# Cross-attention on one core: three score banks, paired value tiles, row sums in a maximum buffer, one transpose for the negated maxima

## What is computed

```python
x = (hidden_states - mu) * jax.lax.rsqrt(var + LN_EPS) * ln_gamma + ln_beta
Q = _split_heads(x @ Wq.T)          # B=2, 32 heads, 512 rows, 32 columns
K = _split_heads(memory_keys)       # 1024 rows; memory_keys = memory_values = ctx_4096
V = _split_heads(memory_values)
scores = jnp.einsum('bhsd,bhtd->bhst', Q, K) * scale
scores = jnp.where(mask, scores, -jnp.inf)
probs = jax.nn.softmax(scores, axis=-1)
attn = jnp.einsum('bhst,bhtd->bhsd', probs, V)
out = attn.transpose(0, 2, 1, 3).reshape(B, S, HIDDEN) @ Wout.T
return residual + out
```

## Time and profile before

| | |
|---|---|
| median of 3 runs | 747.28 us (745.67 to 748.48) |
| the profiled execution's own time | 746.45 us |
| its span | 744.6 us |
| its mean granted TensorE clock | 0.974 |
| busy: PE, DVE, POOL, ACT | 695.1, 483.7, 391.5, 350.1 us |

### The profile page before, as it was taken

One profiled execution on the slowest core, in us unless ns is written; L12 is line 12 of the kernel. 1 busy time (PEld: TensorE's weight loads), 2 busy tenths in 40 slices (PEclk: granted clock), 3 DMA queues, 4 the chain that ended last, 5 costly groups with the idle time before them and its releaser, 6 DMA issues.

```text
span 744.6 us, 10855 instructions
## 1 busy us (share of the span) xinstructions
PE 695.1 (93%) x3585; PEld 400.3 (54%) x3585; DVE 483.7 (65%) x496; ACT 350.1 (47%) x613; POOL 391.5 (53%) x106
## 2 busy tenths in 40 slices
PE   2599999968999999999999999999999999699998
PEld 2478788633444444444444444444444444378886
DVE  6743343148688878878788787887888677732231
ACT  3732111434466666666666566665666666400000
POOL 1000000047296797967979769787796798800000
PEclk9599999979999999999999999999999999989999
DMA  9521000425326144162451523515325104131331
GB/s 346 138 71 57 29 28 1 101 66 127 93 66 156 39 120 115 48 151 52 104 132 50 131 69 89 137 48 127 88 70 128 58 1 135 36 114 57 113 113 56
DMA packets 39518, 68.10 MB, mean 91 GB/s; under 512 B 5284, under 2 KB 21798, under 8 KB 39470
## 3 DMA queue, kind: packets, MB, share of 16 engines
q1 hardware_dynamic: 39444, 67.64, 33.2%
q10 hardware_dynamic: 36, 0.01, 0.0%
HBM read 25.18 MB, written 4.19 MB: 39 GB/s over the span
## 4 chain that ended last, share of the span: by engine, by line
PE 85%; DVE 6%; SPq 5%; DMA 2%; issue 1%; ACT 1%; ACTq 0%; DVEq 0%
PE SX L894 18%; PE MX L874 17%; PE PV L910 16%; PE MX L1038 12%; PE SM L900 6%; PE PV L844 6%; PE SM L844 5%; DVE mx L701 2%; PE MX L821 2%; SPq L301 2%; DVE stats L635 1%; PE MX L815 1%; PE MX L886 1%; SPq L303 1%; DMA PR<-in_x 1%
## 5 line engine op out<-in xcount | busy, mean ns | idle before, releaser
L701 DVE TENSOR_REDUCE mx<-MX 128x1 f32<-128x1024 f32 x256 | 303.0, 1220 | 137.5 <-PE MX L874 137.2
L585 ACT ACTIVATE PR<-SX 128x512 f32<-128x512 f32 x512 | 277.5, 594 | 187.0 <-PE SX L894 186.8
L468 POOL TENSOR_TENSOR acc<-acc,PR 128x2048 f32<-128x2048 f32 x64 | 293.3, 4583 | 31.6 <-ACT PR L585 25.1
L468 POOL TENSOR_TENSOR acc<-PR 128x2048 f32<-128x2048 f32 x16 | 73.3, 4579 | 226.1 <-ACT PR L585 147.6
L894 PE MATMUL SX<-R 99*128 99x512 f32 x512 | 180.2, 432 | 2.4 <-ACT PR L585 1.6
L874 PE MATMUL MX<-R 97*128 97x512 f32 x512 | 164.1, 417 | 14.9 <-DVE mx L701 7.2
L894 PEld LDWEIGHTS SX<-R 99*128 99x128 f32 x512 | 88.4, 189 | 112.0 <-ACT PR L585 91.7
L874 PEld LDWEIGHTS MX<-R 97*128 97x128 f32 x512 | 89.2, 189 | 102.7 <-DVE mx L701 65.0
L910 PE MATMUL PV<-PR,C 128*32 128x512 f32 x1024 | 138.4, 613 | 0.1
L1038 PE MATMUL MX<-R 128*128 128x512 f32 x192 | 46.8, 404 | 5.6 <-DVE R L780 5.6
L789 DVE TENSOR_TENSOR PR<-PR,MX 128x512 f32<-128x512 f32 x16 | 11.0, 687 | 58.6 <-PE MX L1038 57.2
(11 more groups left out here) (75 smaller groups left out, 523.1 us busy)
## 6 DMA issues: line engine op xcount, KB each, us to landing
R<-KTh SPq DMA_DIRECT2D x64, 256.0 KB, 4.2
PR<-in_x SPq DMA_DIRECT2D x16, 512.0 KB, 4.1
C<-in_ctx SPq DMA_DIRECT2D x16, 512.0 KB, 3.5
R<-KTl SPq DMA_DIRECT2D x64, 128.0 KB, 3.8
R<-QT SPq DMA_DIRECT2D x64, 128.0 KB, 2.5
acc<-in_L_xattn_Wq SPq DMA_DIRECT2D x8, 512.0 KB, 3.4
R<-QT SPq DMA_DIRECT2D x64, 64.0 KB, 2.1
C<-in_L_xattn_Wout SPq DMA_DIRECT2D x8, 512.0 KB, 3.3
```

Of the source, the lines that this page charges most:

```text
L468: nc.gpsimd.tensor_tensor(acc[:, :, :], a, PR[:, tt % RING, :, :], ALU.add).then_inc(pool_used, 1)
L585: nc.scalar.activation(PR[:, tt % RING, h, :], SX[h % 2][:, :], ACT.Exp, scale=SCALE).then_inc(exp_done, 1)
L701: nc.vector.tensor_reduce(mx[:, u % 2, c:c + 1], MX[par][:, :], mybir.AxisListType.X, ALU.max, negate=True).then_inc(mx_freed, 1)
```

## The change

- Three score banks SX in turn, (4 tt + h) % 3, in place of two; the third is the bank of SM, which is gone.
- The tables go by slots of two tiles (A, B, C, D in this text: tiles 0 and 1, 2 and 3, 4 and 5, 6 and 7). A slot has its 8 scores in groups of 3, 1, 2 and 2 (`GROUPED`), each with its items behind it, and one value block behind all, with two tiles: 1 and 2, 3 and 4, 5 and 6. Tile 7 of the step before and tile 0 are done at the end of slot A, on both sides of the row sums.
- Row sums are made once per step there, as an item `sums` in an MX buffer: tiles 6 and 7 and `acc` in a row. GpSimd adds tiles 0 to 5.
- The maxima lie in the order in which they are made, so one transpose serves the bias; its rows are 16 x 128 in place of 4 x 512.
- The items are placed anew: the bias item stands at the head of slot D in place of the middle of tile 6, a step makes M6 to M15 for n+1 and M0 to M5 for n+2, in place of M4 to M15 and M0 to M3.

```diff
-POOL_TILES = (0, 1, 2, 4, 5, 6)
+BANKS = 3
+PROBS = TT * HPG
+POOL_TILES = (0, 1, 2, 3, 4, 5)
+DIRECT_TILES = (6, 7)
 ADDS = len(POOL_TILES) - 1
-SUM_SLOT = 1
-FIRST_DIRECT = min(set(range(TT)) - set(POOL_TILES))
+SLOTS = TT // 2
+
+GROUPED = [((0, 0), (0, 1), (0, 2)), ((0, 3),), ((1, 0), (1, 1)), ((1, 2), (1, 3))]
-SUMS_AT = (2, 5, 7)
-LAST_SUMS_AT = (2, 3, 4)
+SUMS_AT = ((1, 0), (1, 1))
...
 STEP = [
-    ([], keys(2)),
-    (maxima(1, 4), maxima(1, 5, 6)),
-    ([], maxima(1, 7, 8)),
-    ([], maxima(1, 9, 10)),
-    (maxima(1, 11), maxima(1, 12, 13)),
-    ([], maxima(1, 14, 15)),
-    ([], maxima(2, 0) + bias(1)),
-    (maxima(2, 1), maxima(2, 2, 3)),
+    (keys(2), maxima(1, 6), maxima(1, 7), maxima(1, 8) + sums(-1)),
+    (maxima(1, 9), maxima(1, 10), maxima(1, 11), maxima(1, 12)),
+    (maxima(1, 13), maxima(1, 14), maxima(1, 15), maxima(2, 0)),
+    (bias(1) + maxima(2, 1), maxima(2, 2), maxima(2, 3), maxima(2, 4, 5)),
 ]
...
-    BTh = sb("BTh", [HPG, S], F32R)
-    BTl = sb("BTl", [HPG, S], F32R)
-
-
-    mx = sb("mx", [P, 2, (ST - 1) * HPG + P], F32)
+    BTh = sb("BTh", [M_ITEMS, P], F32R)
+    BTl = sb("BTl", [M_ITEMS, P], F32R)
+
+
+    mx = sb("mx", [P, 2, P], F32)
...
-    SX = [nc.alloc_psum_tensor(f"SX{i}", [P, S], F32) for i in range(2)]
+    SX = [nc.alloc_psum_tensor(f"SX{i}", [P, S], F32) for i in range(BANKS)]
     PV = nc.alloc_psum_tensor("PV", [P, S], F32)
-    SM = nc.alloc_psum_tensor("SM", [P, S], F32)
-    QP = [PV, SM]
+    QP = [PV, SX[2]]
...
-            def step(n, u, items, at, first=False):
-                for tt in range(TT):
-                    exps(n, u, tt, 0)
-                    if tt == 0 and not first:
+            def step(n, items, at, first=False):
+                for k, slot in enumerate(items):
+                    for group, part in zip(GROUPED, slot):
+                        for b, h in group:
+                            exp(n, 2 * k + b, h)
+                        at = high_and_bias(n, part, at)
+                    if k == 0 and not first:
                         pv_copy(n - 1)
-                    at = high_and_bias(n, items[tt][0], at)
-                    exps(n, u, tt, 1)
-                    at = high_and_bias(n, items[tt][1], at)
...
+                            if kind == "wout":
+                                wout_parts(i, at % 2)
+                            if kind == "max":
+                                maximum(n + a, u + a, i, at % 2)
+                            if kind == "sums":
+                                invert_sums(n + a, 0, MX[at % 2][:, 0:S])
+                                dve.wait_ge(sums_turned, n + a + 1)
+                                dve.sem_inc(mx_freed, 1)
+                            at += 1
+                        if (k, j) in SUMS_AT and not first:
+                            invert_sums(n - 1, 1 + SUMS_AT.index((k, j)))
...
             def bias_item(n, u, par):
-                for st in range(ST):
-                    ins = nc.tensor.transpose(MX[par][:, st * P:(st + 1) * P], mx[:, u % 2, st * HPG:st * HPG + P], ident[:, :])
-                ins.then_inc(bt_ready, 1)
+                nc.tensor.transpose(MX[par][:, 0:P], mx[:, u % 2, :], ident[:, :]).then_inc(bt_ready, 1)
...
+
+                if at >= BANKS:
+                    pe.wait_ge(exp_done, PROBS * n + at - BANKS + 1)
+                elif not is_first(n):
+                    pe.wait_ge(exp_done, PROBS * n - PROBS + max(b for b in range(PROBS) if b % BANKS == at) + 1)
+                elif SX[at] is QP[1]:
+                    pe.wait_ge(q_copied, 2 + BATCH * GROUPS)
...
+            def row_sums(n, bank):
+
+                for tt in DIRECT_TILES:
+                    sum_probs(bank, lambda h: PR[:, tt % RING, h, :], tt == DIRECT_TILES[0], False).then_inc(tile_used, 1)
                 pe.wait_ge(pool_used, ADDS * n + 2 * ADDS)
-                sum_probs(lambda h: acc[:, h, :], False, True).then_inc(sums_done, 1)
+                sum_probs(bank, lambda h: acc[:, h, :], False, True).then_inc(sums_done, 1)
...
+                for k, slot in enumerate(items):
+                    for j, (group, part) in enumerate(zip(GROUPED, slot)):
+                        for b, h in group:
+                            score(n, u, 2 * k + b, h)
+                        if j == len(slot) - 1 and k == 0 and not first:
+                            for item in part[:-1]:
+                                mx_item(*item)
+                            values(n - 1, u + RING - 1, TT - 1)
+                            mx_item(*part[-1])
                         else:
...
+                            for item in part:
+                                mx_item(*item)
+                    if k > 0:
+                        values(n, u, 2 * k - 1)
+                    values(n, u, 2 * k)
...
-            last_sum(STEPS - 1)
+            row_sums(STEPS - 1, SX[0][:, :])
```

192 lines of the change are left out of this document (74 added, 118 removed).

## The result

The changed kernel takes 841.79 us, the median of 4 runs (837.04 to 846.47); the kernel before, run beside it, takes 746.67 us. The ratio is 1.127, with a 95% interval of 1.123 to 1.130: 95 us slower, where 53 were forecast, and 6 us above the range of 768 to 836. The profiled execution took 837.04 us.

The account below looks back on a forecast made before the run. PE was taken as the bound in steps 1 to 13. A step of 34.4 us against 30.3 gave 13 x 4.1 = 53 us on 746.45, so 800 us; forecast 788 to 818, 8-in-10 range 768 to 836.

Parts of the forecast that it names:

- The walk through the slots: One step priced slot by slot: A 10.6, B 6.5, C 6.3, D 9.3, sum 32.7 us, 5.9 of it standstill.
- The standstill behind the keys: Slot A: PE waits 1.4 us for the keys' buffer, until ACT's and DVE's copies of the keys are done.
- the one behind the bias: Slot D: PE stands still 1.8 us before the second item behind the bias, until ACT copies and DVE subtracts.
- M0's wait: Slot C: M0 waits for stacking DMAs queued behind the values' load, 1.0 us plus 0.7 for the load's traffic.
- DVE's split of the queries: Slot A: DVE's splitting of the queries was priced at 3.0 us, keeping DVE busy until 2.8.
- The clock falls as well: Rival: standstills lower PE's clock once to twice in each step, 17 to 34 us more, 817 to 834; chance 0.17.
- the whole block behind each stretch keeps PE busy: Argument against a clock fall after slot D's stretch of half-busy PE, a fall priced at 1.3 us each.
- Step 0 gains fewer borders and meets the same two waits: 0: Step 0: savings at block borders and the waits behind bias and keys were taken to give no net change.
- the clean step: Steps 1 to 13 without M0's wait or clock falls: 32.7 us each, against 30.3 before.
- PE's work: PE's own work in a step after the change, without waits: 26.8 us, 2.6 less than before.
- POOL's chain: Five POOL adds, then exponential, score, item and blocks: 29.3 us a step, deciding if both waits are covered; 731 us, chance 0.08.

Follow-up runs that it names:

- b1: Kernel before with only the bias item moved, from tile 6 to tile 7 right ahead of M1: 796.14 us, ratio 1.067.
- x1: Changed kernel with the values' load placed behind the 16 stacking DMAs in SP's queue: 803.36 us, ratio 1.076.
- x13: x10 with the values' load put back ahead of the stacking DMAs: 791.08 us, ratio 1.059.
- x9: Changed kernel with DVE's split of the queries (cast and subtraction) on one column in place of 512: 840.14 us, ratio 1.125.
- x3: x1 with the bias item also moved to the end of slot C, ahead of the value block: 800.41 us, ratio 1.075.
- x4: x3 with the keys item moved to the end of slot D and M5 to slot A: 821.13 us, ratio 1.100.
- x7: x3 with each maximum over 512 of its 1024 columns, which leaves out work: 785.21 us, ratio 1.051.
- x5: x4 with M0 to M2 placed behind the first eight scores of step 0: 816.64 us, ratio 1.092.
- x12: x10 with each maximum over 512 of its 1024 columns, which leaves out work: 741.87 us, ratio 0.993.
- x10: x5 with the queries split behind M8 of slot A, where POOL is idle, and key rows stacked first: 753.74 us, ratio 1.009.

## Why the prediction was right in sign and wrong in size

**Right: who becomes late.** The walk through the slots held, where the clock doesn't fall. Against 10.6, 6.5, 6.3 and 9.3 stand 10.88, 6.50, 6.39 and 8.82, a step of 32.6 where 32.7 was written. So close a sum is partly luck. The standstill behind the keys was put at 1.4 and is 1.39, but the one behind the bias was put at 1.8 and is 0.88. I had costed the bias rows of 16 x 128 at nothing, with the 0.59 and 0.68 of the old shape; ACT's copy takes 0.25 now and DVE's subtraction 0.28:

```profile
450.20 0.28 DVE L709 TENSOR_TENSOR BTl<-MX,BTh 16x128 fp32r<-16x128 f32 x1 [4.44 <-ACT BTh L550]
```

POOL's first add waits longer, the row sums and their blocks run as one piece of 4.4 (463.21 to 467.64), SP stacks behind the load. b1 shows the slot D standstill to be enough by itself. M0's wait, "1.7" a step, is 2.0 in 12 steps (24.1 us), and x1 and x13 show that it comes from the load's place in SP's queue. Two slips in the working leave the 800 as it is: with 2.6 us of work less in a step that is 2.4 longer, the waiting grows by 5.0 and not 5.5, and a step of 33.7 gives 791 us, not 788.

**One price was wrong without effect.** DVE's split of the queries was put at 3.0 from the earlier trace rows. It takes 1.1 here, because there the cast had stood beside POOL's add (402.92 to 407.49 in the trace of before) and the subtraction beside POOL's multiplication (407.46 to 408.92). I read a wait as work. In steps 1 to 13 of the changed kernel nothing comes of it (x9), but any rearrangement that moves the split back beside an add pays for it (x3, x4, x7).

**Wrong: the clock was a rival, not a term.** The step that failed is the price of the clock, which the sum of 800 puts at nothing; "The clock falls as well" was only a rival, with 0.17 and "17 to 34 us more". It happened, at 32 us, on top of the rest. Without it the same kernel would have come to some 810, inside the range. The size of that rival was right, its place mostly not: it was priced from slot D, where 5.5 of the 32 lie. The argument against it, "the whole block behind each stretch keeps PE busy", failed: in the trace of the changed kernel the block behind the standstill is what runs at the lower clock (3.47 in place of 1.92). I had the row that spoke for it, the 1.43 block in step 0 of before, with 0.67 granted, and weighed it less than I should. The Trainium skill's warning cited there (TensorE: Matmul & The Clock Gate, Why this matters for your kernels) agrees in kind: idle gaps of 2.81 and 0.97 us stand ahead of granted clocks of 0.58 and 0.70. Both gaps are shorter than those that the section names, so here the measurement decides.

**Wrong: "Step 0 gains fewer borders and meets the same two waits: 0".** It costs 7.6. The timeline of PE in step 0 of the changed kernel, the first item of maxima and the first block:

```profile
155.64 1.19 PE L880 MATMUL MX<-R 97*128 97x512 f32 x2 [10.74 <-DMA R<-R]
...
160.18 1.63 PE L920 MATMUL PV<-PR,C 128*32 128x512 f32 x8
```

and that of the kernel before:

```profile
156.00 2.04 PE L874 MATMUL MX<-R 97*128 97x512 f32 x4 [5.52 <-DMA R<-R]
```

M0 comes at the same time in both. But before, PE made tile 1's first scores and value block 0 while it waited, so it stood for 5.5 and not for 10.7, and those are now done afterwards. Behind it the keys' wait is 2.71, since the cast stands beside POOL's first add there (3.60 us). That the order of the first items is the cause is read from these rows and not shown by a run: x5 was made for it and shortens M0's wait to 8.0, but its 4.5 us are those of the split, and its step 0 still takes 53.3. The walk began in step 1 and never looked at which scores stand ahead of M0 in step 0.

**The sum, term by term**, on the profiled spans (+90.6): the clean step 26 (forecast 31: 13 x 2.4, against a mean step of 30.58 and not the 30.32 that one step showed), M0's wait 24 (22), the clock 32 (0), step 0 7.6 (0), the rest 0.9 (0). x1 has 32.75 as a step without a fall, which would move 2 us from the clock to the clean step. The rest to the 95 of the medians is this profiled execution, the fastest of the four.

**The gain that was expected and did not come.** PE's work was put at 26.8 a step and POOL's chain at 29.3, and x12 bears both out, with 27.3 in its step 1 and 29.1 where POOL holds it. x10 has both waits covered and still takes 30.5. In its slot B DVE works without a pause from 422.00 to 427.31 (four maxima and the inversion), then stands until the first item of slot C is made:

```profile
428.50 4.62 DVE L705 TENSOR_REDUCE mx<-MX 128x1 f32<-128x1024 f32 x4 [1.19 <-PE MX L885]
```

With two buffers it has two maxima in stock when PE's block of two tiles starts, and they are worked off before the block, three scores and the next item are done: 5.31 + 1.19 is slot B's 6.50. x7 and x12 show it from the other side, with 5.90 for the slot at half the maxima, and x12 then meets POOL's chain. So pairing the blocks takes work from PE and puts DVE's pause in its place. Shown is that DVE sets slots B to D and that POOL is next; not separated is what each part of the change gives, nor was a third MX buffer tried. x10's step 0 keeps some 8 us: M0 waits 8.5 in place of 5.5, and slot D runs at the lower clock. What would mend it wasn't tried.

## What to carry to other kernels

- When an in-order engine is the bound, ask of every item that needs a round trip through two other engines what long work stands behind it, ahead of the next one that needs its buffer. An item of four transposes moved by a tile cost 50 us (b1), though the move removed nothing and added nothing.
- Give the clock a term of its own in the sum as soon as the walk shows standstills in each step, and price it from the profile's own block durations at the two levels. Walk the first step apart.
- A DMA that waits for late work must not stand ahead of one that is wanted early in the same queue: 37 us here for the order of the two.
